# Four PSUM banks for the maxima rows and two for the scores in a layer's head attention

## The reference

```
def _attn(x, W_qkv, b_qkv, W_ao, b_ao):
    b, s, d = x.shape
    qkv = jnp.einsum('bsd,od->bso', x, W_qkv) + b_qkv
    ...
    scores = jnp.einsum('bhqd,bhkd->bhqk', q, k) * SCALE
    wts = jax.nn.softmax(scores, axis=-1)
    o = jnp.einsum('bhqk,bhkd->bhqd', wts, v)
    o = jnp.moveaxis(o, 1, 2).reshape(b, s, d)
    return jnp.einsum('bsd,od->bso', o, W_ao) + b_ao

for l in range(L):                       # L = 4
    m = _mamba(x, ...)
    x = _ln(x + m, g1[l], be1[l])
    a = _attn(x, W_qkv[l], b_qkv[l], W_ao[l], b_ao[l])
    x = _ln(x + a, g2[l], be2[l])
    h = jax.nn.gelu(...)
    x = x + ...
```

## Time and profile before

| what | value |
|---|---|
| median of 3 runs | 3271.56 us (3259.83 to 3273.29) |
| the profiled execution's own time | 3267.46 us |
| its span | 3265.8 us |
| mean granted TensorE clock | 0.933 |
| PE, DVE, ACT busy | 86%, 57%, 54% of the span |
| L1849, the maxima of the rows | 1024 times 687 ns |
| L1445, the exponentials | 512 times 1024 ns |

### The profile page before, as it was taken

One profiled execution on the slowest core, in us unless ns is written; L12 is line 12 of the kernel. 1 busy time (PEld: TensorE's weight loads), 2 busy tenths in 40 slices (PEclk: granted clock), 3 DMA queues, 4 the chain that ended last, 5 costly groups with the idle time before them and its releaser, 6 DMA issues.

```text
span 3265.8 us, 56810 instructions
## 1 busy us (share of the span) xinstructions
PE 2812.3 (86%) x17396; PEld 1737.5 (53%) x17396; DVE 1863.4 (57%) x3116; ACT 1770.7 (54%) x2669; POOL 805.1 (25%) x864
## 2 busy tenths in 40 slices
PE   7877799787899787898788879999966999799999
PEld 4444446444455444464444446666644777466666
DVE  4567735577546577445677345444536887454444
ACT  6457656367655377654477654444422666544443
POOL 0212200122100222101122014444440000244444
PEclk8989999799899699999799989999987999899999
DMA  2134300244200344101344000000002332000000
GB/s 94 43 94 108 79 6 8 67 100 107 52 12 8 89 103 104 26 8 33 93 99 98 6 7 1 0 0 0 0 1 94 98 101 72 4 4 7 3 6 6
DMA packets 95850, 150.50 MB, mean 46 GB/s; under 512 B 13152, under 2 KB 81248, under 8 KB 89312
## 3 DMA queue, kind: packets, MB, share of 16 engines
q1 hardware_dynamic: 95712, 148.77, 17.3%
HBM read 79.00 MB, written 67.11 MB: 45 GB/s over the span
## 4 chain that ended last, share of the span: by engine, by line
PE 43%; issue 23%; DVE 13%; POOL 11%; DMA 4%; SPq 2%; ACT 2%; DVEq 1%; POOLq 1%; ACTq 0%
POOL hhlo L2179 9%; DVE hmx L1849 9%; PE ps L948 7%; PE ps L754 3%; PE ps L973 2%; PE ps L717 2%; PE ps L681 2%; PE ps L687 2%; PE ps L793 2%; PE ps L829 2%; PE ps L1154 1%; DMA hqk<-hqk_scratch 1%; PE ps L815 1%; SPq L556 1%; DMA hqk_scratch<-hqks 1%
## 5 line engine op out<-in xcount | busy, mean ns | idle before, releaser
L1849 DVE TENSOR_REDUCE hmx<-ps 128x2 f32<-128x512 f32 x1024 | 660.1, 687 | 310.9 <-PE ps L948 310.1
L1445 ACT ACTIVATE hpt<-ps 128x1024 f32<-128x1024 f32 x512 | 522.3, 1024 | 289.5 <-PE ps L960 287.7
L2179 POOL TENSOR_TENSOR hhlo<-hh,hhh 128x512 fp32r<-128x512 f32 x320 | 414.8, 1296 | 463.0 <-ACT hhh L1524 462.1
L948 PE MATMUL ps<-hqk 24*128 24x256 f32 x2048 | 309.0, 359 | 235.1 <-DVE hmx L1849 189.1
L948 PEld LDWEIGHTS ps<-hqk 24*128 24x128 f32 x2048 | 191.5, 206 | 461.8 <-DVE hmx L1849 412.1
L1519 ACT ACTIVATE sil<-ps 128x512 f32<-128x512 f32 x320 | 191.0, 597 | 441.4 <-PE ps L1156 437.4
L1943 DVE TENSOR_TENSOR su<-ps,sil 128x512 f32<-128x512 f32 x256 | 177.1, 692 | 326.7 <-PE ps L1156 318.4
L973 PE MATMUL ps<-hpt,hvx 128*32 128x256 f32 x4096 | 299.3, 413 | 1.9 <-ACT hpt L1445 1.6
L960 PE MATMUL ps<-hqk 26*128 26x256 f32 x2048 | 272.2, 348 | 1.7 <-ACT hpt L1445 1.2
L1524 ACT ACTIVATE hhh<-hh 128x512 fp32r<-128x512 f32 x320 | 199.5, 624 | 40.9 <-DVE hh L1946 26.8
L2136 POOL CAST hqks<-hqk 128x512 fp32r<-128x512 f32 x64 | 40.5, 633 | 673.3 <-ACT hqk L1425 641.8
(11 more groups left out here) (247 smaller groups left out, 5593.1 us busy)
## 6 DMA issues: line engine op xcount, KB each, us to landing
hqk_scratch<-hqks SPq DMA_DIRECT2D x256, 192.0 KB, 3.1
hqk<-hqk_scratch SPq DMA_DIRECT2D x256, 192.0 KB
qk_scratch<-qks SPq DMA_DIRECT2D x16, 768.0 KB, 3.3
k<-qk_scratch SPq DMA_DIRECT2D x16, 384.0 KB
qv<-qk_scratch SPq DMA_DIRECT2D x64, 96.0 KB
mw<-mw_in SPq DMA_DIRECT2D x10, 516.5 KB, 3.9
w12raw<-w_in SPq DMA_DIRECT2D x1, 2560.0 KB, 9.5
streams<-x_in SPq DMA_DIRECT2D x8, 256.0 KB, 4.8
```

The lines of the kernel that those rows point to most:

```text
L948: return mm(ps[:, o % 2, qt * SEQ:(qt + 1) * SEQ], hqk[r][32 * g:32 * g + 24, 0, j, qt * P:(qt + 1) * P], hqk[r][32 * g:32 * g + 24, 1, j, ...
L1445: A(hpt[:, j, g:g + 2, :, :], ps[:, 2 + g:4 + g, :], ACT.Exp, scale=QSCALE).then_inc(hd_exp, 1)
L1849: V.tensor_reduce(hmx[:, r, :, 4 * g + j], ps[:, o % 2, :].rearrange("p (t k) -> p t k", t=2), AX.X, ALU.max).then_inc(hd_max, 1)
L2179: G_.tensor_tensor(hhlo[:, k % 4, :], hh[:, k % 2, :], hhh[:, k % 4, :].bitcast(F32), ALU.subtract).then_inc(e_lo, 1)
```

## The change

Rows used banks 0 and 1 (`o % 2`) and scores banks 2 to 5 (`2 + g`, with g the head's place in its group of four). Now rows use banks 0 to 3 (`o % 4`) and scores banks 4 and 5. So a pair of rows waits for the maxima two pairs back, not one pair back, and a pair of scores waits for the exponential one step back, not two.

```diff
-                    return mm(ps[:, o % 2, qt * SEQ:(qt + 1) * SEQ],
+                    return mm(ps[:, o % 4, qt * SEQ:(qt + 1) * SEQ],
...
-                    pe.wait_ge(hd_max, nth(hd_max, l * BATCH + b, o - 2))
+                    pe.wait_ge(hd_max, nth(hd_max, l * BATCH + b, o - 4))
...
-                    return mm(ps[:, 2 + g, kt * SEQ:(kt + 1) * SEQ],
+                    return mm(ps[:, 4 + g % 2, kt * SEQ:(kt + 1) * SEQ],
...
-                        pe.wait_ge(hd_exp, nth(hd_exp, B, p - 2))
+                        pe.wait_ge(hd_exp, nth(hd_exp, B, p - 1))
                         if both:
-                            pe.wait_ge(hd_max, nth(hd_max, B + ahead, o - 1))
+                            pe.wait_ge(hd_max, nth(hd_max, B + ahead, o - 3))
...
-                    A(hpt[:, j, g:g + 2, :, :], ps[:, 2 + g:4 + g, :], ACT.Exp, scale=QSCALE).then_inc(hd_exp, 1)
+                    A(hpt[:, j, g:g + 2, :, :], ps[:, 4:6, :], ACT.Exp, scale=QSCALE).then_inc(hd_exp, 1)
...
-                    V.tensor_reduce(hmx[:, r, :, 4 * g + j], ps[:, o % 2, :].rearrange("p (t k) -> p t k", t=2), AX.X,
+                    V.tensor_reduce(hmx[:, r, :, 4 * g + j], ps[:, o % 4, :].rearrange("p (t k) -> p t k", t=2), AX.X,
```

## The result

| | before | changed |
|---|---|---|
| median of 12 runs | 3263.89 us | 3282.97 us |
| lowest and highest | 3252.89 and 3273.29 | 3268.14 and 3292.65 |
| ratio, with 95% interval | | 1.005 [1.0034, 1.0065] |
| the profiled execution, its span | 3267.46, 3265.8 | 3285.43, 3283.8 |
| mean granted TensorE clock | 0.933 | 0.924 |

The change makes the kernel slower by half a percent, 19 us. I had forecast about no change. The time lies in my range, near its upper end; the direction was not the one that I held likeliest.

What follows compares the result with a forecast made beforehand. It took a PE-DVE ring of 1.88 us a step as the bound, with a second chain through spill and maxima DMA. Terms -20.7 - 3 + 12 + 11 = -0.7 on 3267.5 gave about 3267, written as 3269 us; range 3248 to 3292.

Steps and rivals of the forecast that it cites:

- The ring: Full steps: PE waits for the previous step's exponential, 1.76 us from even to odd step and 1.83 from odd to even.
- The sequence: 44 steady sequences, closed by the DMA of the maxima: 15.07 us each instead of 15.54, a gain of 20.7 us.
- Sequences 0 and 1: Sequences 0, 1, 13 and 14, sixteen in all: 0.2 us gained each, 3 us, between 0 and 7.
- The last sequence of each layer: Where no rows are left, each exponential waits for its own scores: 3.0 us slower a layer, 12 us, bounds 6 and 20.
- The clock: PE idle before step 0 lowers its clock in one of six of 44 sequences: 11 us lost, bounds 0 and 70.
- The second: Rival: clock falls at most sequence starts, 1.6 us each, slower from 18 falls of 44 on; chance 0.1.
- The first: Rival: the clock stays up, its term is 0, sum -12, or -18 (3253 us) without the register wait; chance 0.2.
- the third: Rival: sequences stay at 15.5 us because the DMA wait takes 11.9 each time, 3279 to 3290 us; chance 0.15.
- What the sum was: Whole kernel: sequence, first sequences, layer ends and clock together give -0.7 us against the profiled execution, about 3267.
- A sign that I read wrongly: Steady sequences, steps 1 to 7: PE's rows should be released by ACT or the DMA, not by DVE.

Runs made afterwards that it cites:

- e2: Changed kernel, but odd-step scores use banks 2 and 3 where no rows are left, so PE runs two steps ahead there again; 3255.4 us.
- e3: Changed kernel plus a wait for DVE's maxima and two extra 128 by 128 matmuls on PE at the end of step 7; 3267.9 us.
- e8: Changed kernel plus a wait for DVE's maxima and one extra 128 by 128 matmul on PE at the end of step 7; 3267.2 us.
- e10: Changed kernel plus only the wait for DVE's maxima at the end of step 7, without extra matmuls; 3283.8 us.
- e11: Kernel before, banks untouched, plus one 32 KB DMA on SP between the spill and the maxima, so the maxima go later; 3281.2 us.
- e5: Changed kernel with the edits of e2 and e3 together; 3237.6 us.
- e12: e5 plus a wait for DVE's maxima and four more extra matmuls in step 2 of sequences 13 and 14; 3220.8 us.
- e7: Changed kernel with the spill in two DMAs instead of four, same bytes; 4277.2 us, 1.31 times the kernel before.

## Why the prediction was wrong, step by step

- **The ring.** Right. I had PE step to PE step at 1.76 and 1.83; the profile has 1.76 and 1.84 for the first four distances. The 0.07 that I added for the register wait is there: PE moves 0.13 after the exponential, as against 0.12 in my sum.
- **The sequence.** Right. I had 3.59 + 11.48 = 15.07; it is 15.02 to 15.04, with medians of 3.59 and 11.44. 37 of the 44 closed on the DMA of the maxima. Against the median sequence the gain is 18.5 us where I had 20.7. The bounds that I wrote, 14.95 and 15.62, do not come out of my own terms, which give 3.45 + 11.44 = 14.89 and 3.73 + 11.96 = 15.69; nothing hangs on it.
- **Sequences 0 and 1.** A gain of 6.2 us, and 1.4 for 13 and 14: 7.6 where I gave 3, just outside my bound of 7. Right in direction.
- **The last sequence of each layer.** This failed: "I take 3.0 a layer, 12 us". Sequence 15 lasts 15.2 to 16.8 us instead of 9.9 (I had said near 13), which is 23.8 us in the profile, and e2 takes 27 us off the median. I had worked the step at the full clock, 1.61. In the trace the first distances are 1.62 and 1.70, and then the clock falls (at 418.1), after which PE's own work bounds the step at 2.6 and more. With the second step of lead back (e2) it stays up through sequence 15 in three of the four layers, so the idle time between the steps is the likely cause of these falls. My upper bound of 20 named this case, and I did not take it; what was measured lies above even that.
- **The clock.** This failed too: "If one in six of the 44 is hit" gave 7 falls and 11 us. There were 15 falls, one in three, with 16 long sequences, and 22.2 us more above the median than before. The price, 1.6 us, was right (24.7 / 16 = 1.5). The count was not, and I misread the trace that I had. I wrote that most sequences that closed on the DMA before were followed by no fall. These are the six starts of step 0 before at which PE waited for the DMA:

```profile
212.66 0.38 PE L948 MATMUL ps<-hqk 24*128 24x256 f32 x2 [0.51 <-DMA hqk<-hmt]
...
710.68 0.38 PE L948 MATMUL ps<-hqk 24*128 24x256 f32 x2 [0.99 <-DMA hqk<-hmt]
...
1158.94 0.38 PE L948 MATMUL ps<-hqk 24*128 24x256 f32 x2 [0.50 <-DMA hqk<-hmt]
...
1176.03 0.38 PE L948 MATMUL ps<-hqk 24*128 24x256 f32 x2 [1.33 <-DMA hqk<-hmt]
...
1192.33 0.38 PE L948 MATMUL ps<-hqk 24*128 24x256 f32 x2 [0.51 <-DMA hqk<-hmt]
...
1640.51 0.38 PE L948 MATMUL ps<-hqk 24*128 24x256 f32 x2 [0.74 <-DMA hqk<-hmt]
```

  The clock's records fall at 1161.3, 1178.4 and 1642.6, behind the third, the fourth and the sixth: three of six. In the changed kernel it is 14 of 37, and once more behind a start that names DVE. "Every sequence closes on the DMA" and the rate of these six would have given 22 falls, too many; one in six was too few.
- **Which of the two weighs more.** In the profiles they miss by the same, 12 and 11 us. In the timed runs the last sequences are the surer miss: e2 takes 27 us off the median (25 by the ratio) where I had 12, while e3 and e8 take 15 and 16 us off (10 and 12 by the ratios) where I had 11 for the clock. Neither alone puts the time where it is.
- **The rivals.** The second (falls at most starts) had the mechanism but set its turning point at 18 falls; with the larger loss at the end 15 were enough. The first, that the clock stays up, is ruled out by the 15 falls, and the third, that the sequence gets no shorter, by the 15.04.
- **What the sum was.** -20.7 - 3 + 12 + 11 stood at -0.7. With what was measured, and -1.8 for all else, it is -18.5 - 7.6 + 23.8 + 22.2 - 1.8 = +18.1; the two profiled executions differ by 18.0.
- **A sign that I read wrongly.** I had said that DVE should no longer be named as the releaser of the rows. The waits still name it often, since its reductions end almost together with the exponentials; the starts at 0.13 after the exponential are what tells. Releasers are inferred.

The Trainium skill, "TensorE: Matmul & The Clock Gate", section "A second HAM failure mode: psum-queue depth-cycling", tells of brief idle spells that make the clock swing and cost throughput. The traces agree (15 falls and 13 in the changed kernel and e10, 1 in e3); e11 shows that it is the idle spell, not the choice of banks. The same page of the Trainium skill, section "HAM oscillation — how this bites in real kernels", tells of a kernel in which double-buffering in PSUM gained nothing; here the deeper buffer did shorten the clean sequence, from 15.46 to 15.04, and e5 brings that gain out.

## What to carry to other kernels

When a wait is taken away and another ends the loop, more of the engine's idle time gathers at that one place (here 0.31 us ahead of step 0 became 0.52), and on TensorE that can cost as much as the shorter loop gains: look at the granted clock behind each such wait before counting the gain. One or two useless matmuls in the gap, into a bank that a later step overwrites, bought 15 us on the changed kernel (10 to 12 by the ratios), and four more in each of two sequences at the end of the layers another 17 (e12 against e5; 15 by the ratios). When banks are moved from one ring to another, look at the stages in which only one of the two runs; there the spared banks can be lent back.

## What the runs showed of the hardware

- One 128 by 128 float32 matmul in 15 us made the difference between 15 or 13 falls of the clock and one (e8 against the changed kernel and e10), in one profiled execution of each. PE's idle time ahead of step 0 was 0.29 us with it and 0.52 and 0.51 without.
- DMAs of 384 KB with 64 partitions held SP's queue for 6.4 us a pair, and the next small DMAs for 9.7 us, while four of 192 KB with 32 partitions took 2.57 us for the same bytes (e7).
- PE moves 0.13 us after an exponential whose wait stands on a register instruction ahead of the matmul (median of 191 starts in the changed kernel), and 0.05 us after one where the matmul's own wait is for the exponential (24 starts where no rows are left) or, before the change, for DVE (436 starts).
